# Early-fusion transformer block on one core: query and key products in two places a step, other PSUM banks for token values, contexts and projection

## The chip, the core and the metric

The kernel runs on one NeuronCore of a Trainium2 chip. TensorE (PE) multiplies matrices into PSUM, ScalarE (ACT) and VectorE (DVE) read PSUM and write SBUF, GpSimd (POOL) and SyncE (SP) mostly issue DMAs and do small work. Each engine runs its own instructions in order, and engines wait for one another through semaphores. The metric is the device time of one execution in microseconds; less is better.

## The reference

```python
h = tok(x)                       # 256x256 image, 3 channels: colour matrix, curve, mix, clip to 0..1
h = concat([h, txt], axis=1)     # 8 batches x 384 tokens x 256
h = h + attn(layernorm(h))       # 16 heads of 16, causal, latent keys and values
h = h + ffn(layernorm(h)) + bias # 8 experts, top 2, capacity 384 rows, gelu, 256 -> 1024 -> 256

def attn(x):
    c = x @ W_DKV                # latent, 64 wide
    k, v, q = c @ W_UK, c @ W_UV, x @ W_UQ
    s = q @ k.T * 0.25, masked causally
    return softmax(s) @ v @ W_O
```

## The kernel before

The program has two stages. The first (`front`) does tokens, attention and routing for 8 batches of 384 tokens; the second (`experts`) does the feed-forward part. The change is in `front` alone.

**Turns and steps.** A batch has 16 heads in two halves of 8. A turn `n` treats half `n % 2` of batch `n // 2`; it has four steps `p`, of two heads each. In a step PE computes, in this order: scores of the next turn for the row maxima, group 0 (L604, 8 matmuls with their masks), shifted scores of this turn unit 0 (L626), place A, shifted scores unit 1, scores group 1, the middle place, shifted scores unit 2, and the end place. ACT takes the exponential of each shifted unit (L917, L919), DVE reduces each group of scores to row maxima (L1111) and PE may not write a group again before DVE has read it. At places A, middle and end stands everything else, spread by hand over the steps: PE, ACT, DVE and SP each have a loop over `n` and `p` with the same ifs, and each engine's order is the order of the code. "Odd turn" and "even turn" below mean the parity of `n`.

**Queries and keys.** q and k are split in three bf16 parts each, so that their products can be taken exactly enough in bf16. `query_key(b, k, stage)` does it in three stages: stage 0 multiplies in fp32 (queries L720, `k` even; keys L722, `k` odd), ACT copies the result to `part` as bf16 (L978); stage 1 and 2 subtract the last part inside PSUM by a product with minus the identity (L725) and ACT copies again. So 12 products and 12 copies a batch make one chain, since from batch 2 on all use the same PSUM bank (`M[1]`, the third bank of `t_bank`): a product waits for the copy before it. In the code before, they stand in all three places of the steps: two of the chain in odd step 1, three each in odd steps 2 and 3 and in even step 0, the last in even step 1. SP sends each part on to the stacked tiles `qs` and `ks` (L392).

**The single banks.** `M[0]` (`bank0`) serves the transposes of the row maxima (`maxima`, L635), one half of the token values (L732, 2 tiles), contexts out of an odd turn (L681), the projection (`project`, L690) and the transposed rows for the router (`rows_back`, L740). `M[1]` serves tokens back (L698), latents (L705), the query and key chain, the other half of the token values (1 tile) and contexts out of an even turn. `take` makes PE wait until the last reader of a bank is done.

**Other work in the places.** ACT has colours (L953) in odd steps, relus (L962) in even steps 0 and 1; DVE has the rest of the colours, the token curve (L1162, L1166), norms, routing and residual additions (L1145).

Of the kernel before, what the change touches and what calls it, by code (L numbers as in the profile page):

```python
# [30 lines left out]
B = 8  # L31
# [110 lines left out]
def front(nc, common, lent, wr, w_in, routed, x, txt, params, mats, w1, w2, slot_rows, out):  # L142
# [8 lines left out]
    ident, banks, s_bank, t_bank, buf, sem = common  # L151
# [7 lines left out]
    def live(b):  # L159
        return 0 <= b < B  # L160
# [4 lines left out]
    def late(b):  # L165

        return 2 <= b < B
# [179 lines left out]
        return C[:, T:T + NT * KE] if b < B - 2 else s_bank[:, 1, 0:NT * KE]  # L347

    def project_bank(b, k):
        return s_bank[:, 2, :] if b == B - 1 and k else M[0]  # L350

    def rows_bank(b, c):
        return M[1] if b == B - 1 and c else M[0]
# [2 lines left out]
    EARLY_ORDER = (((0, 0), (1, 0), (2, 0), (0, 1), (1, 1), (3, 0), (0, 2), (1, 2), (2, 1), (3, 1), (2, 2), (3, 2)),  # L356
                   tuple((k, i) for half in ((0, 1), (2, 3)) for i in range(3) for k in half))
    EARLY_BANKS = (("s0", "s1", "s2", "t0"), (1, "C", 1, "C"))

    def bank_of(key):  # L360
        if key == "C":
# [32 lines left out]
    def sync(sp):  # L394
# [36 lines left out]
        for n in range(FIRST, LAST):  # L431
            b = n // 2
            if n % 2 == 0:
                if b + 1 == 1:
                    for i in range(3):
                        for k in (2, 3):
                            stack(sp, 1, k, i)
                elif live(b + 1):
                    for i in range(3):
                        stack(sp, b + 1, 3, i)  # L440
                if live(b + 2) and live(b + 4):
                    load_x(b + 4)
                if live(b - 2):
                    store(b - 2)
                if b + 2 == B:
                    sp.wait_ge(tok_done, B)
                    for i, w in enumerate(weight_layouts(w1, w2, 0)):
                        sp.dma_start(wr[i][:, :].rearrange("p (c f) -> p c f", f=w.shape[2]),
                                     w).then_inc(w_in[i], 16)
            else:  # L450
                if b + 2 == 1:
                    for i in range(3):
                        for k in (0, 1):
                            stack(sp, 1, k, i)
                    load_x(3)
                elif live(b + 2):
                    for k in range(3):
                        for i in range(3):
                            stack(sp, b + 2, k, i)
            if 0 <= n < PIECES:  # L460
                empty_rows(n)
# [121 lines left out]
    def tensor(pe):  # L583
        last = {}
# [58 lines left out]
        def take(bank, reader, count):  # L643

            release(bank)
            last[bank] = [(reader, count)]
# [36 lines left out]

        def project(b, k):
            pe.wait_ge(cn_sb, 2 * b + 2)
            take("last" if b == B - 1 and k else 0, hid_add, 2 * b + k + 1)
            dst = project_bank(b, k)
            for at, t in enumerate((0, 1) if k == 0 else (2,)):
                for c in range(KC):
                    mm = pe.matmul(dst[:, at * DIM:(at + 1) * DIM], cn[:, c, t * P:(t + 1) * P], wo[:, c, :],  # L690
                                   start=(c == 0), stop=(c == KC - 1))
            mm.then_inc(wo_ps, 1)
# [94 lines left out]
        for n in range(FIRST, LAST):  # L787
            b, odd = n // 2, n % 2
            nxt, cur, prev = turn_live(n + 1), turn_live(n), turn_live(n - 1)
            for p in range(4):  # L790
# [23 lines left out]
                        contexts_back(n, 0, False)  # L814
                if odd and p == 1 and late(b + 2):
                    latents(b + 2, 1)
                if odd and p >= 2 and late(b + 2):
                    query_key(b + 2, p - 2, 2)
                if not odd and p < 2 and late(b + 1):
                    query_key(b + 1, 2 + p, 2)  # L820

                if n == FIRST and p == 3:
                    for k in (0, 1):
# [10 lines left out]
                    for k in (2, 3):  # L834
                        query_key(1, k, 1)

                if odd and late(b + 2):
                    if p == 0:
                        tokens_back(b + 2, 0, 1)
                    else:  # L840
                        query_key(b + 2, p - 1, 0)
                if not odd and p == 0 and late(b + 1):
                    query_key(b + 1, 3, 0)
                if p == 0 and prev:
                    values(n - 1, 1)
                if p == 2 and cur:
# [1 line left out]
                if odd:  # L848
                    if p == 0 and live(b - 1) and n < OVER:
                        project(b - 1, 1)  # L850
                    if p == 3 and live(b - 1):
                        rows_back(b - 1, 0)
                else:
                    if p == 1 and live(b + 1):
                        token_values(b + 1, 0, 0)
                    if p == 3 and live(b - 1):
                        project(b - 1, 0)
                    if p == 3 and n == OVER:
                        ranks(b - 2)
                        project(b - 1, 1)  # L860
                        turning(50)
# [4 lines left out]
                if odd:  # L866
                    if p == 2 and prev:
                        contexts_out(n - 1, 0)
                    if late(b + 2):
                        if p == 0:  # L870
                            tokens_back(b + 2, 1, 1)
                        else:
                            query_key(b + 2, p - 1, 1)
                    if n == FIRST and p == 0:
                        for c in range(KC):
                            tokens_back(1, c, c)
# [5 lines left out]
                    if p == 3 and live(b - 1):  # L882
                        rows_back(b - 1, 1)
                else:
                    if p == 0 and late(b + 1):
                        query_key(b + 1, 3, 1)
                    if p == 1 and live(b + 1):
                        token_values(b + 1, 1, 1)
                    if p == 2 and prev:
                        contexts_out(n - 1, 1)  # L890
                        if n == OVER:
                            turning(20)
                    if n == OVER and p == 0:
# [6 lines left out]
    def scalar(act):  # L900
# [116 lines left out]
        for n in range(FIRST, LAST):  # L1017
            b, odd = n // 2, n % 2
            nxt, cur, prev = turn_live(n + 1), turn_live(n), turn_live(n - 1)
            for p in range(4):  # L1020
                if p == 3 and prev:
                    contexts_out(n - 1, 0 if odd else 1)
                if odd and p == 1 and late(b + 2):
                    tokens_back(b + 2, 1, 1)
                if odd and p >= 2 and late(b + 2):
                    query_key(b + 2, p - 2, 1)
                if not odd and p < 2 and late(b + 1):
                    query_key(b + 1, 2 + p, 1)
                if cur:
                    exps(n, p, 0)  # L1030

# [3 lines left out]
                    maxima(n + 1, 0)  # L1035
                if odd and p == 1 and late(b + 2):
                    latents(b + 2, 1)
                if odd and p >= 2 and late(b + 2):
                    query_key(b + 2, p - 2, 2)
                if not odd and p < 2 and late(b + 1):  # L1040
                    query_key(b + 1, 2 + p, 2)
                if n == FIRST and p == 3:
                    for k in (0, 1):
                        query_key(1, k, 1)
# [9 lines left out]
                if p == 2 and nxt:  # L1054
                    max_rows(n + 1, 0)

                if odd and late(b + 2):
                    if p == 0:
                        tokens_back(b + 2, 0, 1)
                    else:  # L1060
                        query_key(b + 2, p - 1, 0)
                if not odd and p == 0 and late(b + 1):
                    query_key(b + 1, 3, 0)
                if n == 0 and p == 0:
                    for k in (2, 3):
                        query_key(1, k, 1)
# [10 lines left out]
                    contexts(n - 1, 1)  # L1077
                if p == 2 and cur:
                    contexts(n, 0)
                if not odd and p == 0 and live(b + 2):  # L1080
                    relus(b + 2, 0)
                if not odd and p == 1 and live(b + 1):
                    token_values(b + 1, 0, 0)
                    token_values(b + 1, 1, 1)
                if n == FIRST and p == 0:
                    for c in range(KC):
                        tokens_back(1, c, c)
# [641 lines left out]
```

## Time and profile before

| what | value |
|---|---|
| time, median of 3 runs | 706.63 us (704.95 to 707.01) |
| profiled execution, its time | 704.81 us |
| profiled execution, its span | 703.1 us |
| PE busy | 639.8 us (91%) |
| DVE busy | 400.3 us (57%) |
| ACT busy | 377.8 us (54%) |
| POOL busy | 305.5 us (43%) |

The span is divided in two: attention up to some 380 us, experts from some 402 us on. The turns that hold a query and key chain of a late batch (2 to 7) lie between 60 and 320 us. In the rows of the timeline a row is one group of equal instructions; its second number is how long it was busy, and in brackets at its end stands how long the engine had been idle and what released it. The busy time of a matmul overlaps with the next one's.

### The profile page before, as it was taken

How to read it: one execution, taken by the hardware profiler on the slowest of the kernel's cores; microseconds unless marked ns; L12 is line 12 of the kernel's file. 1: busy time of each engine (PE TensorE's matmuls, PEld its weight loads, DVE VectorE, ACT ScalarE, POOL GpSimd, SP SyncE). 2: the span in 40 equal slices, each digit the busy share in tenths (PEclk: the TensorE clock that was granted, in tenths of full speed). 3: DMA queues.
4: the chain of work that ended last, by engine and by line, in shares of the span. 5: the costliest groups of instructions: out<-in, count | busy, mean ns of one | idle time of the engine just before them, and what ended most of it. 6: DMA issues, size and time to landing. Idle time of an engine off the chain costs nothing.

```text
span 703.1 us, 14382 instructions
## 1 busy us (share of the span) xinstructions
PE 639.8 (91%) x5488; PEld 533.9 (76%) x5488; DVE 400.3 (57%) x1005; ACT 377.8 (54%) x800; POOL 305.5 (43%) x415
## 2 busy tenths in 40 slices
PE   2799899998999999999988699999999999999991
PEld 2556565665666657567667699999999999999990
DVE  4887585687777877757766353444444444444310
ACT  4466766747667576565561265555555554555530
POOL 3300001004121141220426497888888888888222
PEclk9999999999999999999999889999999999999996
DMA  7448391714424043153103443444444444442222
GB/s 260 113 119 230 97 269 52 199 47 134 118 68 131 9 112 93 56 144 129 63 17 103 127 143 76 106 106 106 106 106 106 106 106 106 106 106 47 23 25 28
DMA packets 66477, 73.76 MB, mean 105 GB/s; under 512 B 6312, under 2 KB 61458, under 8 KB 66408
## 3 DMA queue, kind: packets, MB, share of 16 engines
q1 hardware_dynamic: 55584, 59.27, 27.8%
q0 software_dynamic: 9504, 13.00, 10.9%
q8 instruction: 44, 0.72, 0.5%
q10 hardware_dynamic: 1320, 0.57, 0.3%
q14 instruction: 25, 0.20, 0.1%
HBM read 31.62 MB, written 22.35 MB: 77 GB/s over the span
## 4 chain that ended last, share of the span: by engine, by line
PE 67%; DVE 12%; ACT 7%; issue 5%; DMA 3%; SPq 3%; POOL 1%; ACTq 0%; DVEq 0%; POOLq 0%
PE t_bank L1654 19%; PE bank L1669 12%; PE s_bank L1669 6%; PE bank L662 5%; DVE mx L1111 3%; PE t_bank L626 3%; PE t_bank L720 3%; SPq L392 3%; PE s_bank L604 3%; ACT part L978 2%; PE bank L690 2%; PE s_bank L1640 2%; DVE wr L1166 2%; PE t_bank L627 1%; PE s_bank L605 1%
## 5 line engine op out<-in xcount | busy, mean ns | idle before, releaser
L1613 DVE TENSOR_TENSOR hl<-h,hh 128x384 fp32r<-128x384 f32 x128 | 104.5, 818 | 155.7 <-ACT h L1571 155.7
L1111 DVE TENSOR_REDUCE mx<-s_bank 128x2 f32<-128x256 f32 (+2 forms) x192 | 122.6, 683 | 51.9 <-PE s_bank L605 51.3
L1568 ACT ACTIVATE hh<-t_bank 128x384 fp32r<-128x384 f32 x128 | 63.0, 492 | 133.9 <-PE t_bank L1654 131.7
L919 ACT ACTIVATE pt<-t_bank 128x512 f32<-128x512 f32 x128 | 76.8, 601 | 65.8 <-PE t_bank L627 64.8
L1538 POOL DMA_INDIRECT out<-yo,xr x48 | 75.0, 1564 | 72.6 <-ACT yo L1579 62.9
L1526 POOL TENSOR_TENSOR wl<-wr,wh 128x256 fp32r<-128x256 f32 x112 | 94.5, 878 | 1.2
L1654 PE MATMUL t_bank<-xh,wh 128*128 128x384 f32 x256 | 87.2, 341 | 0.0
L1654 PE MATMUL t_bank<-xl,wh 128*128 128x384 f32 x256 | 86.8, 339 | 0.0
L1654 PE MATMUL t_bank<-xh,wl 128*128 128x384 f32 x256 | 86.7, 338 | 0.0
L626 PE MATMUL t_bank<-qs,ks 98*128 98x384 bf16 (+2 forms) x384 | 85.2, 274 | 0.6 <-ACT pt L917 0.4
L604 PE MATMUL s_bank<-ks,qs 96*128 96x128 bf16 (+2 forms) x384 | 78.3, 273 | 5.4 <-DVE mx L1111 4.6
L520 POOL DMA_INDIRECT slot_rows<-row,slot_i x48 | 47.9, 997 | 73.9 <-ACT pt L919 47.7
L605 PE MATMUL s_bank<-mask_q,ident_b 128*128 128x128 bf16 x384 | 74.4, 219 | 0.0
L1669 PE MATMUL bank<-wh,hh 128*128 128x256 f32 x256 | 72.9, 285 | 0.0
L1669 PE MATMUL bank<-wh,hl 128*128 128x256 f32 x256 | 72.0, 281 | 0.0
L1669 PE MATMUL bank<-wl,hh 128*128 128x256 f32 x256 | 71.8, 280 | 0.0
L627 PE MATMUL t_bank<-mask_k,ident_b 128*128 128x128 bf16 x384 | 68.0, 219 | 0.0
L1571 ACT ACTIVATE h<-t_bank 128x384 f32<-128x384 f32 x128 | 62.3, 487 | 0.0
L626 PEld LDWEIGHTS t_bank<-qs,ks 98*128 98x128 bf16 x384 | 37.6, 98 | 24.0 <-issue 5.3
L502 POOL TENSOR_TENSOR ve<-mv,eps_t 128x3 f32<-128x3 f32 x8 | 1.5, 191 | 123.6 <-DVE mv L1201 123.6
L978 ACT ACTIVATE part<-t_bank 128x384 bf16<-128x384 f32 x78 | 38.1, 488 | 29.0 <-PE t_bank L720 16.9
L1654 PEld LDWEIGHTS t_bank<-xh,wh 128*128 128x128 f32 x256 | 49.4, 193 | 0.0
(191 smaller groups left out, 1433.6 us busy)
## 6 DMA issues: line engine op xcount, KB each, us to landing
wr<-in_w SPq DMA_DIRECT2D x16, 1024.0 KB, 5.7
qs<-part SPq DMA_DIRECT2D x96, 96.0 KB
ks<-part SPq DMA_DIRECT2D x90, 96.0 KB
slot_rows<-empty SPq DMA_DIRECT2D x4, 1560.0 KB, 9.3
xr<-slot_rows SPq DMA_DIRECT2D x16, 390.0 KB, 3.3
wr<-in_x SPq DMA_DIRECT2D x8, 768.0 KB, 5.4
out<-hid SPq DMA_DIRECT2D x8, 384.0 KB
qs<-mT ACTq DMA_DIRECT2D x64, 3.0 KB
```

Of the source, the lines that this page charges most:

```text
L604: pe.matmul(dst, q[0:MROW, h, j * P:(j + 1) * P], k[0:MROW, h, 0:w], start=True, stop=False)
L605: mm = pe.matmul(dst[:, j * P:(j + 1) * P], ident_b[:, :], mask_q[:, :], start=False, stop=True)
L626: pe.matmul(bank[:, col:col + w], k[:, h, j * P:(j + 1) * P], q[:, h, j * P:T], start=True, stop=False)
L627: mm = pe.matmul(bank[:, col:col + P], ident_b[:, :], mask_k[:, :], start=False, stop=True)
L919: ins = act.activation(pt[:, p, unit // 2, 0:AT[1]], bank, ACT.Exp)
L1111: ins = dve.tensor_reduce(mx[:, p // 2, j, 2 * (p % 2):2 * (p % 2) + 2], pair_region(s_bank, j), AX_X, ALU.max)
L1526: m = pool.tensor_tensor(wl[i][q][:, cols], wr[i][:, cols], wh[i][q][:, cols].bitcast(F32), ALU.subtract)
L1538: pool.indirect_dma_start(out=out, out_offset=bass.IndirectOffsetOnAxis(ap=xr[u % NX][:, t, DIM:DIM + 1].bitcast(I32), axis=0), in_=yo[u % ...
L1568: act.activation(hh[:, f, :], h_banks[f % NH], ACT.Gelu_apprx_tanh)
L1613: dve.tensor_tensor(hl[:, f, :], h[f % 2][:, :], hh[:, f, :].bitcast(F32), ALU.subtract).then_inc(hl_done, 1)
L1654: m = pe.matmul(h_banks[f % NH], w[:, c, cols], xx[:, c, :], start=(i == 0), stop=(i == len(parts) - 1))
L1669: m = pe.matmul(y_banks[t], hx[:, f, rows], w[:, f, :], start=(f == 0 and i == 0), stop=(f == FC - 1 and i == 2))
```

## The change

A function `ahead(n, p, place)` numbers the products of a chain over six steps: place 0 is place A, place 1 is the middle place. Odd step 1 has product 0 (middle), odd steps 2 and 3 and even steps 0, 1 and 2 have two each, even step 3 has the last (place A). The end place has none any more. ACT's copies follow: place 0 behind the exponential of unit 0, place 1 behind that of unit 1, none at the head of a step. Token values now both use `M[0]`: tile pair 0 at the end of even step 0, tile 2 in the middle of even step 1. Contexts out always use `M[0]`, the first half of each projection always `M[1]`. SP sends the parts of `k` 2 and 3 in the even turn, those of `k` 0 and 1 in the odd turn.

```diff
     def project_bank(b, k):
-        return s_bank[:, 2, :] if b == B - 1 and k else M[0]
+        if k == 0:
+            return M[1]
+        return s_bank[:, 2, :] if b == B - 1 else M[0]
...
+    def ahead(n, p, place):
+
+        b = n // 2 + (2 if n % 2 else 1)
+        i = 2 * p + place + (-3 if n % 2 else 5)
+        return (b, *divmod(i, 3)) if late(b) and 0 <= i < 12 else None
...
# sync
                 elif live(b + 1):
-                    for i in range(3):
-                        stack(sp, b + 1, 3, i)
+                    for k in (2, 3):
+                        for i in range(3):
+                            stack(sp, b + 1, k, i)
...
                 elif live(b + 2):
-                    for k in range(3):
+                    for k in (0, 1):
                         for i in range(3):
                             stack(sp, b + 2, k, i)
...
# tensor
-            take("last" if b == B - 1 and k else 0, hid_add, 2 * b + k + 1)
+            take(1 if k == 0 else "last" if b == B - 1 else 0, hid_add, 2 * b + k + 1)
...
-                if odd and p >= 2 and late(b + 2):
-                    query_key(b + 2, p - 2, 2)
-                if not odd and p < 2 and late(b + 1):
-                    query_key(b + 1, 2 + p, 2)
+                if ahead(n, p, 0):
+                    query_key(*ahead(n, p, 0))
...
-                if odd and late(b + 2):
-                    if p == 0:
-                        tokens_back(b + 2, 0, 1)
-                    else:
-                        query_key(b + 2, p - 1, 0)
-                if not odd and p == 0 and late(b + 1):
-                    query_key(b + 1, 3, 0)
+                if odd and p == 0 and late(b + 2):
+                    tokens_back(b + 2, 0, 1)
+                if ahead(n, p, 1):
+                    query_key(*ahead(n, p, 1))
...
-                        token_values(b + 1, 0, 0)
+                        token_values(b + 1, 1, 0)
...
-                    if late(b + 2):
-                        if p == 0:
-                            tokens_back(b + 2, 1, 1)
-                        else:
-                            query_key(b + 2, p - 1, 1)
+                    if p == 0 and late(b + 2):
+                        tokens_back(b + 2, 1, 1)
...
-                    if p == 0 and late(b + 1):
-                        query_key(b + 1, 3, 1)
-                    if p == 1 and live(b + 1):
-                        token_values(b + 1, 1, 1)
+                    if p == 0 and live(b + 1):
+                        token_values(b + 1, 0, 0)
                     if p == 2 and prev:
-                        contexts_out(n - 1, 1)
+                        contexts_out(n - 1, 0)
```

The same is done in ACT's loop (copies, token values, contexts out).

On ACT, this is what stands before in an odd turn from the first copy of the chain (step 1) to the contexts (step 2): `pt` is an exponential, `part01` the copy behind stage 1 of product group `k` = 0, `g` a colour, `mT` the row maxima, `cx` the contexts.

```order
L978 ACTIVATE part00<-t_bank 128x384
L919 ACTIVATE pt<-t_bank 128x512
L953 ACTIVATE g<-wr0,prm 128x512
L978 ACTIVATE part01<-t_bank 128x384
L919 ACTIVATE pt<-t_bank 128x512
L926 ACTIVATE mT<-bank0 8x384
L978 ACTIVATE part02<-t_bank 128x384
L917 ACTIVATE pt<-t_bank 128x2x256
L931 DMA qs00<-mT 1x4x384 x2
L978 ACTIVATE part10<-t_bank 128x384
L919 ACTIVATE pt<-t_bank 128x512
L939 ACTIVATE cx<-bank1 128x384
```

And this is what stands there now (the line numbers of ACT's code are one lower):

```order
L977 ACTIVATE part00<-t_bank 128x384
L918 ACTIVATE pt<-t_bank 128x512
L952 ACTIVATE g<-wr0,prm 128x512
L918 ACTIVATE pt<-t_bank 128x512
L925 ACTIVATE mT<-bank0 8x384
L977 ACTIVATE part01<-t_bank 128x384
L916 ACTIVATE pt<-t_bank 128x2x256
L930 DMA qs00<-mT 1x4x384 x2
L977 ACTIVATE part02<-t_bank 128x384
L918 ACTIVATE pt<-t_bank 128x512
L938 ACTIVATE cx<-bank1 128x384
```

The copy between the colour and the next step's first exponential is gone; the two others of the step are there still, and hold the members of the chain that stood one place earlier.

On PE, this is the order before from the middle place of even step 1 to the beginning of step 2: `L732` is a product of token values, `L626` and `L627` a shifted unit.

```order
L732 MATMUL bank0<-mat,ckvT 128x256 x2
L626 MATMUL t_bank<-qs10,ks10 128x384
L627 MATMUL t_bank<-mask_k,ident_b 128x128
L626 MATMUL t_bank<-qs10,ks10 128x128
L627 MATMUL t_bank<-mask_k,ident_b 128x128
L732 MATMUL t_bank<-mat,ckvT 128x256
L604 MATMUL s_bank<-ks11,qs11 128x128
```

And this is the order now (the line numbers of PE's code are nine higher):

```order
L734 MATMUL t_bank<-part21,minus_b 128x384
L741 MATMUL bank0<-mat,ckvT 128x256
L635 MATMUL t_bank<-qs10,ks10 128x384
L636 MATMUL t_bank<-mask_k,ident_b 128x128
L635 MATMUL t_bank<-qs10,ks10 128x128
L636 MATMUL t_bank<-mask_k,ident_b 128x128
L613 MATMUL s_bank<-ks11,qs11 128x128
```

The pair of token values has gone to the end of step 0, a subtraction of the chain stands in its place, and step 1 ends with the shifted unit.

## Rows read from the trace of the kernel before

**Rows 1.** The page: span, and TensorE's clock in 40 slices.
```profile
span 703.1 us, 14382 instructions
...
PEclk9999999999999999999999889999999999999996
```
**Rows 2.** Odd, even turn: length; busy PE, PEld, DVE, ACT, POOL; clock; DMA.
```profile
146.90:170.98 24.08, 21.65 (x197) 14.18 (x196) 17.27 (x60) 14.91 (x32) 6.26 (x8) 1.00 0.25 67
170.98:191.70 20.72, 19.75 (x198) 14.22 (x196) 16.55 (x47) 13.97 (x30) 4.06 (x5) 1.00 0.47 129
```
**Rows 3.** PE's waits from 60 to 400 us: total us, times, longest.
```profile
PE t_bank L725 <- ACT part L978: 5.5, 13, 0.7
PE t_bank L722 <- ACT part L978: 4.1, 12, 0.6
PE bank L635 <- DVE hid L1145: 3.6, 6, 0.7
PE s_bank L604 <- DVE mx L1111: 3.3, 5, 0.7
```
**Rows 4.** PE's waits from 30 to 60 us.
```profile
PE bank L635 <- ACT vb L987: 1.0, 1, 1.0
```
**Rows 5.** Timeline of PE and ACT, odd steps 1 and 2.
```profile
157.91 0.22 PE L627 MATMUL t_bank<-mask_k,ident_b 128*128 128x128 bf16 x1
158.22 0.59 ACT L919 ACTIVATE pt<-t_bank 128x512 f32<-128x512 f32 x1
158.38 0.34 PE L725 MATMUL t_bank<-part,minus_b 128*128 128x384 bf16 x1 [0.24 <-ACT part L978]
158.55 0.22 PE L604 MATMUL s_bank<-ks,qs 96*128 96x128 bf16 x1
158.69 0.81 ACT L953 ACTIVATE g<-wr,prm 128x512 f32<-128x512 f32 x1
159.40 0.49 ACT L978 ACTIVATE part<-t_bank 128x384 bf16<-128x384 f32 x1
...
160.12 0.60 ACT L919 ACTIVATE pt<-t_bank 128x512 f32<-128x512 f32 x1 [0.23 <-issue]
160.62 0.46 ACT L926 ACTIVATE mT<-bank 8x384 bf16<-8x384 bf16 x1
160.74 0.22 PE L605 MATMUL s_bank<-mask_q,ident_b 128*128 128x128 bf16 x1
160.99 0.46 ACT L978 ACTIVATE part<-t_bank 128x384 bf16<-128x384 f32 x1
161.59 0.88 PE L722 MATMUL t_bank<-ckvT,mat 128*128 128x384 f32 x2 [0.63 <-ACT part L978]
162.41 0.53 PE L662 MATMUL bank<-pt,vb 128*32 128x384 f32 x4
```
**Rows 6.** Timeline of DVE and PE at the beginning of an odd turn.
```profile
147.33 0.68 DVE L1145 TENSOR_TENSOR hid<-hid,bank 128x512 f32<-128x512 f32 x1
148.15 0.33 PE L635 MATMUL bank<-ident_b,ms 128*8 128x128 bf16 x3 [0.74 <-DVE hid L1145]
```
**Rows 7.** Timeline of PE and DVE in even steps 1 to 3.
```profile
180.05 1.08 PE L732 MATMUL bank<-mat,ckvT 128*128 128x256 f32 x4
180.97 0.33 PE L626 MATMUL t_bank<-qs,ks 98*128 98x384 bf16 x1
185.58 1.88 DVE L1111 TENSOR_REDUCE mx<-s_bank 128x2 f32<-128x256 f32 x3
186.93 0.23 PE L604 MATMUL s_bank<-ks,qs 96*128 96x128 bf16 x1 [0.69 <-DVE mx L1111]
```
**Rows 8.** Timeline of PE, the two transposes of rows, odd step 3.
```profile
169.26 0.49 PE L740 MATMUL bank<-ident,row 128*128 128x128 f32 x3
170.00 0.34 PE L725 MATMUL t_bank<-part,minus_b 128*128 128x384 bf16 x1
170.47 0.52 PE L740 MATMUL bank<-ident,row 128*128 128x128 f32 x3
```

More of the change, by code:

```diff
@@ L1021, in scalar @@
                 if p == 3 and prev:
-                    contexts_out(n - 1, 0 if odd else 1)
+                    contexts_out(n - 1, 0)
                 if odd and p == 1 and late(b + 2):
                     tokens_back(b + 2, 1, 1)
[L1025 to L1028, printed above, removed]
                 if cur:
@@ L1037, in scalar @@
                     latents(b + 2, 1)
[L1038 to L1041, printed above, removed]
+                if ahead(n, p, 0):
+                    query_key(*ahead(n, p, 0))
                 if n == FIRST and p == 3:
@@ L1055, in scalar @@
                     max_rows(n + 1, 0)
[L1057 to L1063, printed above, removed]
+                if odd and p == 0 and late(b + 2):
+                    tokens_back(b + 2, 0, 1)
+                if ahead(n, p, 1):
+                    query_key(*ahead(n, p, 1))
+                if not odd and p == 1 and live(b + 1):
+                    token_values(b + 1, 1, 0)
                 if n == 0 and p == 0:
@@ L1079, in scalar @@
                     contexts(n, 0)
+                if not odd and p == 0 and live(b + 1):
+                    token_values(b + 1, 0, 0)
                 if not odd and p == 0 and live(b + 2):
                     relus(b + 2, 0)
-                if not odd and p == 1 and live(b + 1):
-                    token_values(b + 1, 0, 0)
-                    token_values(b + 1, 1, 1)
                 if n == FIRST and p == 0:
```

## The prediction

> **What bounds the kernel now.** I read the page first: PE's clock stands at 9 tenths or more in every slice of attention [rows 1], so no pause there has cost clock. Then two stretches, one odd and one even turn of a late batch [rows 2]: PE is busy 21.65 of 24.08 us and 19.75 of 20.72, DVE 17.27 and 16.55, ACT 14.91 and 13.97. So PE sets the pace, DVE is the next, and what the change can give is at most the time in which PE waits. Then PE's waits between 60 and 400 us [rows 3]: 9.6 us in 25 waits for ACT's copies of the query and key chain (5.5 + 4.1), 3.6 us in 6 waits of the row maxima's transposes for DVE's residual addition, 3.3 us in 5 waits for DVE's maxima. One wait of 1.0 us for the token values of batch 1 stands before [rows 4].
>
> These sums are too small, since the modelled end of a matmul overlaps with the next start. The L627 at 157.91 is followed at a distance of 0.06 us when nothing holds PE, so L725 could have started at 157.97; it started at 158.38 [rows 5]. The wait is 0.41 us and the view says 0.24: add 0.17 to each wait. The Trainium skill, page "Perfetto Trace Analysis", section "Identifying the Most-Contended Engine", says in the same sense that matmul busy time misleads because instructions are pipelined; by busy time alone the 25 waits would be worth 9.6 us, by the distance of starts 13.9. By that rule the trace agrees (0.41 against 0.24).
>
> **The change, part by part.** Amount of work: every engine has the same products, copies and reductions as before, in other places; SP issues the same DMAs. The sum is therefore the waits that go less the waits that come.
>
> *Projection in the other bank.* In odd step 0 `maxima` needs `bank0`, in which the projection's first half lies until DVE has added it. The addition starts at 147.33, takes 0.68, and PE starts at 148.15 after 0.74 idle [rows 6]. Now that half is in `M[1]`. Six waits go: 3.6 + 6 x 0.17 = 4.6 us. `M[1]` is next wanted by tokens back in the middle place, behind a transpose and two more groups of products, when the addition is done. Late next is the projection itself: it needs the bank in which the last subtraction of the chain was made two groups of products earlier, and its copy. Subtraction to end of copy is about 0.9 us (L725 at 159.94 before its copy at 160.99 is held up by others, so I take 0.36 to start, 0.49 for the copy at 159.40 [rows 5], 0.07 to wake PE), the work between is 0.85: 0.07 each, 0.4 in all. Gain 4.2. Bounds: 0 (another wait takes its place) and 4.6.
>
> *The chain at odd step 2.* Work from the row of the last exponential of step 1, at 158.22, called X. Before, ACT has a colour at 158.69, a copy at 159.40, an exponential, `mT`, and the copy that PE needs at 160.99; PE goes on at 161.59. PE's last product ahead of it, L605 at 160.74, is followed at 0.06 us when free, so this wait is 0.79; and 0.41 was lost at 158.38 [rows 5]. Now ACT's line is exponential (0.47 to the colour), colour (0.71 to the next), exponential (0.50), `mT` (0.37), copy 0.46, and 0.11 until PE starts: X + 2.62. PE no longer subtracts at the end place; it needs 158.55 to 160.80 = 2.25 us for the same groups from 157.97 = X - 0.25, and is there at X + 2.00. It waits 0.62. Over six batches 3.7 us stay.
>
> *The chain at even step 0.* The same form (exponential, `mT`, copy). The mean wait of L722 is 4.1 / 12 + 0.17 = 0.51. ACT loses the copy at the step's head (about 0.40), PE the subtraction ahead of the step (L725 to L604, 158.38 to 158.55, 0.17 [rows 5]), so 0.51 - 0.40 + 0.17 = 0.28 stays: 1.7 us over six.
>
> *The rest of the chain.* From the middle place to place A of the next step lie a shifted unit, the next scores and another shifted unit, more than the 0.9 us that a copy takes; the waits at odd step 3 (the largest, 0.7 [rows 3]) go, because nothing is copied at the head of a step behind colour and contexts any more. From place A to the middle place lie a shifted unit and a group of scores: about 0.05 us each in 18 cases, 0.9 us. So the chain's waits go from 9.6 + 25 x 0.17 = 13.9 to 3.7 + 1.7 + 0.9 = 6.3: gain 7.6. Bounds: 3 (ACT is behind its line in every step, so that half of the pairs wait 0.5 us) and 13.9.
>
> *Even turns and DVE.* In even step 3 PE waits for maxima that DVE reads late (185.58), until 186.93, 0.69 + 0.17 = 0.86 us [rows 7]. DVE works on without a pause from the maxima of step 1 through routing and the token curve, so this time does not move with PE. PE arrives later by what has come between: less the pair of token values (180.05 to 180.97, 0.92 [rows 7]), plus two subtractions (0.17 each) and one key product (161.59 to 162.41, 0.82 [rows 5]), 0.24 us. Four of the five waits of [rows 3] lie in such turns: gain 1.0. Bounds: -1 (the curve comes later, since ACT's relus now stand behind one more copy; it has about 1.5 us to spare) and 3.4.
>
> *Rows back.* In odd step 3 the second transpose needs the copy of the first. They are 1.21 us apart (169.26, 170.47), and a subtraction at 170.00 fills 0.17 of it [rows 8]. That subtraction leaves, the distance stays: 5 x 0.17 = 0.9 us lost. Bounds 0 and -2.
>
> *Token values.* For batch 1 the wait of 1.0 + 0.17 [rows 4] goes, since tile 2's copy stands ahead of an exponential and not behind it; ACT is then later by 0.4: gain 0.7, bounds 0 and 1.2. For the others the bank is free a step ahead.
>
> *SP.* Parts of `k` = 2 are sent up to two steps later, the image load and the store wait behind them in the same queue. The stacked tile of `k` 2 and 3 is read a whole turn later (over 20 us [rows 2]), the image two turns later: 0. If one were late, some 2 us a batch.
>
> Sum: 4.2 + 7.6 + 1.0 - 0.9 + 0.7 = **12.6 us**. The profiled execution took 704.81 us (span 703.1 and 1.7 around it), so 692.2. The median of the runs is 706.63, 1.8 above it; I give the time from there: **694.0**.
>
> A place where the skill would say more: "TensorE: Matmul & The Clock Gate", section "A second HAM failure mode: psum-queue depth-cycling", tells of a kernel in which small pauses between groups in changing banks made the clock fall and rise, and by it fewer pauses would give back clock too. Here the clock is granted at 1.00 (2.4 GHz) in both stretches [rows 2] in spite of six or seven pauses in each pair, so the trace disagrees and nothing is added.
>
> **The rivals.**
> *ACT gives it back.* With two copies in a step beside three exponentials ACT may be behind at each place A. For it: ACT's line in rows 5 is full from 158.22 to 161.45. Against it: busy only 14.91 of 24.08. Then the chain keeps some 11 of its 13.9 us, and the gain is 4.2 + 3 - 1 = 6: 700.5.
> *All waits go.* PE's arrival in even step 3 is later than reckoned, and ACT is early: 4.6 + 11 + 3 = 18.5 less 1: 689 or a bit less. For it: each small wait ahead of step 3 hides in the one for DVE. Against it: ACT's line X + 2.62 is fixed by in-order work.
> *Slower: odd turns do not shrink.* The change moves two subtractions and a query product (0.17 + 0.17 + 1.37, the last estimated from twice the key product less the pause) from the odd into the even turn, 1.7 us. If the odd turn's length is set by DVE and ACT handing colours to each other and not by PE, it stays at 24.08 while the even turn, where DVE works without a pause, grows: 6 x 1.7 = 10.3, less the 1.5 that rows 6 and 7 leave: 715. It decides where DVE's 17.27 us meet the new length of the odd turn, 24.08 - 1.7 - 2.3 = 20.1; so 2.8 us of room speak against it.
> *No change.* The freed time is lost again before the experts' stage, which starts on routed rows that DVE, POOL and a DMA deliver in sequence: 706. Against it: this sequence starts from the last turn's products, and comes earlier with them.
>
> **How the numbers follow.** A measurement tells 0.3% (2.1 us) from no change. Forecast (690 to 698): 0.62; ACT gives it back (698 to 704): 0.15; all waits go (below 690): 0.09; no change: 0.06; slower: 0.08. Faster is 0.62 + 0.15 + 0.09 = 0.86, same 0.06, slower 0.08. The range 688 to 702 leaves out the slower case, no change and the edges of two others, some 0.2.
>
> **What would show it.** After the change: no wait of `maxima` for `hid`; a wait for ACT's copy at the middle place of odd step 2 of some 0.45 in the view, less than 0.2 elsewhere; a wait for DVE's maxima at even step 3 of some 0.45; a wait of 0.3 at the second rows back; odd turns near 20.2 us, even turns near 22.5, a pair near 42.7 (44.80 before). The prediction is wrong if odd turns stay above 22 us, if the waits for `part` sum to more than 8 us, or if ACT's exponentials hold PE at L626.

## The result, and the profile after

| | before | after |
|---|---|---|
| time, median | 705.79 us (703.58 to 707.01, 4 runs) | 694.45 us (692.97 to 694.65, 4 runs) |
| profiled execution, its time and span | 704.81, 703.1 us | 694.65, 692.9 us |
| ratio of the times | | 0.9845, 95% interval 0.9821 to 0.9869 |

The changed kernel is faster by 11.3 us in the medians and by 10.2 us from profile to profile. The page of its profiled execution, span and TensorE's clock, answers to [rows 1]:

```profile
span 692.9 us, 14382 instructions
...
PEclk9999999999999999999999899999999999999996
```

There are as many instructions as before and the clock stands as high: only waits can have gone. One odd and one even turn, with the columns of [rows 2]:

```profile
143.10:163.99 20.89, 20.09 (x198) 13.78 (x196) 17.55 (x57) 14.04 (x30) 6.45 (x8) 1.00 0.33 102
163.99:186.10 22.11, 21.32 (x200) 14.82 (x198) 17.63 (x52) 14.40 (x31) 4.06 (x5) 1.00 0.37 100
```

These stretches and those of [rows 2] are not cut at the same product: the odd stretch before starts behind the turn's first group of scores and the even one ends with the next turn's, while those above start and end at the first scores. From the first product of scores of one turn to that of the next (turns 5 and 6) it is 24.60 and 20.26 us before, 20.96 and 21.81 after. So the odd turn is shorter by 3.6 us, the even one longer by 1.55, the pair 42.77 for 44.86. DVE is now busy in 17.55 of 20.89 us of the odd turn, where it was in 17.27 of 24.08. PE's waits from 60 to 400 us, as in [rows 3] (total, times, longest):

```profile
PE s_bank L1631 <- DMA xr<-slot_rows: 6.1, 2, 3.6
PE bank L749 <- ACT rowT L990: 2.8, 7, 0.5
PE t_bank L734 <- ACT part L977: 2.3, 6, 0.4
PE t_bank L729 <- ACT part L977: 2.1, 6, 0.4
PE s_bank L613 <- DVE mx L1102: 1.6, 6, 0.5
```

The waits for ACT's copies of the chain (`part`) went from 9.6 us in 25 to 4.4 us in 12, the waits for `hid` are gone, those for the maxima `mx` fell from 3.3 to 1.6 us. (L1631 is the experts' first product, which waits for a DMA and now lies inside the window.) The waits of the transposed rows for their copy (`rowT`) grew; before, that row was

```profile
PE bank L740 <- ACT rowT L991: 0.8, 2, 0.5
```

What is left at odd step 2, against [rows 5]; columns are start, busy time, engine, line:

```profile
239.95 0.59 ACT L918 ACTIVATE pt<-t_bank 128x512 f32<-128x512 f32 x1
240.43 0.81 ACT L952 ACTIVATE g<-wr,prm 128x512 f32<-128x512 f32 x1
241.13 0.60 ACT L918 ACTIVATE pt<-t_bank 128x512 f32<-128x512 f32 x1
241.61 0.46 ACT L925 ACTIVATE mT<-bank 8x384 bf16<-8x384 bf16 x1
241.98 0.46 ACT L977 ACTIVATE part<-t_bank 128x384 bf16<-128x384 f32 x1
242.50 0.34 PE L734 MATMUL t_bank<-part,minus_b 128*128 128x384 bf16 x1 [0.40 <-ACT part L977]
```

From the exponential X = 239.95 ACT works without a gap, and PE goes on at X + 2.55 after 0.40 + 0.17 = 0.57 us. Even step 3, against [rows 7], and the two transposes of rows, against [rows 8]:

```profile
222.93 1.88 DVE L1102 TENSOR_REDUCE mx<-s_bank 128x2 f32<-128x256 f32 x3
224.27 0.23 PE L613 MATMUL s_bank<-ks,qs 96*128 96x128 bf16 x1 [0.23 <-DVE mx L1102]
...
247.90 0.49 PE L749 MATMUL bank<-ident,row 128*128 128x128 f32 x3
249.12 0.52 PE L749 MATMUL bank<-ident,row 128*128 128x128 f32 x3 [0.39 <-ACT rowT L990]
```

The wait for the maxima is 0.40 us where it was 0.86. The transposes are 1.22 us apart, as before (1.21), with no product of the chain between them.

**A mark in attention.** Two runs of one kernel differ by up to 3.5 us, most of it behind attention (last section). So I also compare each kernel by the start of the last transposes of row maxima (turn 15, step 0), a row that every kernel has. Before:

```profile
356.58 0.33 PE L635 MATMUL bank<-ident_b,ms 128*8 128x128 bf16 x3 [0.19 <-DVE hid L1145]
```

After:

```profile
346.28 0.33 PE L644 MATMUL bank<-ident_b,ms 128*8 128x128 bf16 x3
```

The gain at this mark is 10.3 us. The same transposes in each turn split it by pairs of turns (odd and following even): turns 1 and 2 gained 2.03, 3 and 4 2.03, 5 and 6 2.09, 7 and 8 1.84, 9 and 10 1.84, 11 and 12 0.50, turns 13 to 15 up to the mark 0.27. "Steady pair" means turns 9 and 10 below: 44.56 us before, 42.72 after.

The mark has a scatter of its own. Turn 1 starts 0.29 us later after the change than before, but so do the very first transposes of this kind (38.17 before, 38.47 after): it is not turn 0 that lost it. Ahead of them PE waits for a DMA, and that wait was 0.65 to 1.41 us long in the traces, also in kernels with the same code up to there. Before, and in `e_sp`:

```profile
32.54 0.22 PE L604 MATMUL s_bank<-ks,qs 96*128 96x128 bf16 x1 [0.83 <-DMA qs<-part]
33.27 0.22 PE L605 MATMUL s_bank<-ks,qs 96*128 96x128 bf16 x1 [1.41 <-DMA qs<-part]
```

From the first transposes to the mark the change gains 10.6 us. Counted so, the kernels of the next section gain over the one before: `e_bank` 4.3, `e_places` 8.95, `e_mt` 13.4, `e_sp` 0.1, `e_tv` 10.7, `e_curve` 12.3, `e_rows` 13.5, `e_all` 12.4, `e_best` 13.8, `e_dve` 16.8, `e_three` 7.9. Each is one trace.

### The profile page after: what moved, and what is told of

Its sections match the earlier page's. It is cut to its first block, busy times and chain, and to the rows that moved or that the text cites. A ratio compares the mean times of both kernels' runs of the same rounds, so it can differ in the third digit from the quotient of the medians.

```text
span 692.9 us, 14382 instructions
## 1 busy us (share of the span) xinstructions
PE 637.3 (92%) x5488; PEld 533.1 (77%) x5488; DVE 400.3 (58%) x1005; ACT 375.7 (54%) x800; POOL 306.7 (44%) x415
## 4 chain that ended last, share of the span: by engine, by line
PE 70%; DVE 8%; ACT 7%; issue 4%; DMA 4%; SPq 3%; POOL 2%; ACTq 1%; DVEq 0%; POOLq 0%
PE t_bank L1645 19%; PE bank L1660 12%; PE s_bank L1660 6%; PE bank L671 5%; PE t_bank L635 4%; PE s_bank L613 4%; PE t_bank L729 3%; SPq L400 3%; PE t_bank L699 2%; DMA qs<-part 2%; PE t_bank L636 2%; PE s_bank L614 2%; ACT part L977 2%; DVE mx L1102 2%; PE s_bank L1631 2%
## 5 line engine op out<-in xcount | busy, mean ns | idle before, releaser
L1604 DVE TENSOR_TENSOR hl<-h,hh 128x384 fp32r<-128x384 f32 x128 | 101.6, 794 | 158.1 <-ACT h L1562 158.1
```

The costliest lines, as they stand in the source:

```text
L1604: dve.tensor_tensor(hl[:, f, :], h[f % 2][:, :], hh[:, f, :].bitcast(F32), ALU.subtract).then_inc(hl_done, 1)
```

## The experiments

Each ratio is to the kernel before on the same chip (medians there 704.5 to 704.8 us), with its 95% interval. The mark is the row named above, 356.58 before and 346.28 after.

**The bank alone** (`e_bank`): the kernel before, with the projection's first half in `M[1]`.

```diff
     def project_bank(b, k):
-        return s_bank[:, 2, :] if b == B - 1 and k else M[0]
+        if k == 0:
+            return M[1]
+        return s_bank[:, 2, :] if b == B - 1 else M[0]
```

> The kernel before, with one part of the change: the first half of every projection in M[1], so that bank0 is free for the transposes of the row maxima at the head of an odd turn. Theory (six waits for DVE's residual addition go, each 0.60 us in the view and 0.17 more by the distance of starts): 4.6 us less than before, about 701.2 us against 705.8, ratio 0.9935, and no wait of L635 for hid. Rival (another wait takes its place in the same turn, since DVE is behind there without a pause): less than 1 us.

Measured: 701.13 us, ratio 0.995 (0.9931 to 0.9969), mark 352.33. It gains 4.25 at the mark, near the 4.6 expected, and the waits for `hid` are gone; the chain's stay (5.5 us in 13, 4.0 in 12), and so do those for the maxima (3.2 in 5). So it acts on that one wait.

**The places alone** (`e_places`): the changed kernel with the lines above undone.

> The changed kernel with that part undone: the chain in two places a step, token values and contexts as changed, but the projection's first half in bank0 again. Theory: the waits of the row maxima's transposes for hid come back, 0.6 to 0.8 us in each of six odd turns: 4 to 5 us more than the changed kernel, about 699 us, ratio to before 0.990. Rival (the two parts overlap: with the longer even turn DVE's addition is done in time, and the bank is worth little there): within 1 us of the changed kernel, 695.

Measured: 695.84 us, 0.9879 (0.9856 to 0.9902), mark 347.78. The places alone gain 8.8 us at the mark; the bank on top of them only 1.5. My expectation of 699 was wrong for that reason; the rival named beside it (695, the bank worth under 1 us) came nearer. Its waits:

```profile
PE bank L642 <- DVE hid L1134: 2.5, 5, 0.6
PE t_bank L732 <- ACT part L975: 2.3, 6, 0.4
PE t_bank L727 <- ACT part L975: 2.1, 6, 0.4
```

Five waits for `hid` are left, each shorter: in the steady pair 0.81 us before and 0.65 here, and at turn 3 0.54 before and 0.09 here (distances of starts). DVE's addition moves with the longer even turn, but PE comes later still: from the transposes at the start of the even turn to the addition it was 20.14 us before (281.31) and 21.46 here (273.21), and PE was free for its own next transposes 20.15 and 21.63 us behind the same point. At turn 3 these are 18.38 and 18.67 before, 19.23 and 19.95 here.

What the other banks of token values and contexts are worth inside the places was not run, except for batch 1 (`e_tv`).

**ACT's order** (`e_mt`): the changed kernel, with the copy that PE waits for ahead of the copy `mT` on ACT.

```diff
-                if p == 0 and cur:
-                    maxima(n, 1)
-                if p == 2 and nxt:
-                    maxima(n + 1, 0)
...
                     query_key(*ahead(n, p, 0))
+                if p == 0 and cur:
+                    maxima(n, 1)
+                if p == 2 and nxt:
+                    maxima(n + 1, 0)
```

> The changed kernel with one order on ACT turned: the copy of the chain's product of place A stands ahead of the copy of the row maxima (mT) and not behind it, in odd step 2 and even steps 0 and 2. Theory (what is left of the chain's waits is ACT's line exponential, mT, copy): the copy is 0.37 us earlier in each of 12 places where PE waits 0.57 and 0.52 us now, so 4.4 us less than the changed kernel, about 690 us, and the waits for part fall to 0.2 us or out of the view. Rival (DVE sets the turn now): PE only waits later for DVE's maxima, less than 1 us gained. Second rival: the row maxima's DMAs come 0.5 us later and hold the shifted scores: slower.

Measured: 691.16 us, 0.9799 (0.978 to 0.9819), mark 343.50. No other kernel of the study that computes everything was faster by the median (`e_rows` is level with it). It gains 2.8 us at the mark and 3.3 by the median over the change, where 4.4 were expected. All 12 waits for `part` left the list of 60 to 400 us, and others came:

```profile
PE s_bank L613 <- DVE mx L1102: 2.9, 8, 0.5
PE bank L749 <- ACT rowT L990: 2.8, 7, 0.5
...
PE bank L683 <- ACT cx L938: 1.3, 3, 0.5
```

The maxima hold PE for 1.6 us more (1.3 in the view and two waits more at 0.17), the contexts for 1.1 more. The list hides that the chain's pauses are shorter and not gone. By the distance of starts, those of more than 0.12 us ahead of the chain's products fell from 9.5 us in 29 to 4.0 in 23; in the steady pair the two large ones went from 0.57 and 0.52 to 0.23 and 0.17, that in even step 2 (0.28) fell below 0.12, and the pair shrank by 0.37. 5.5 - 1.6 - 1.1 = 2.8, the gain at the mark. So the copies behind `mT` were on the path, and the waits for DVE's maxima and for ACT's copies of contexts take back a half.

**SP's order alone** (`e_sp`): the kernel before, with the parts of `k` 2 sent in the even turn.

```diff
-                    for i in range(3):
-                        stack(sp, b + 1, 3, i)
+                    for k in (2, 3):
+                        for i in range(3):
+                            stack(sp, b + 1, k, i)
```

> The kernel before with SP's part of the change alone: it sends the parts of k = 2 in the even turn, ahead of those of k = 3, and the image load and store behind them. Theory: nothing reads the stacked tile or the image for a turn, so no change, ratio 1.000 within 0.002. Rival (a DMA lands late): about 1 us or more slower.

Measured: 704.45 us, 0.9991 (0.998 to 1.0002), mark 356.99: no change. The 0.4 us at the mark comes from the longer wait ahead of turn 0 shown above; from the first transposes on it is 318.27 us for 318.41.

**Token values of batch 1** (`e_tv`): the changed kernel, with these products and copies in turn 0 where and in the banks that they had before.

```diff
                     if p == 1 and live(b + 1):
-                        token_values(b + 1, 1, 0)
+                        if n == 0:
+                            token_values(b + 1, 0, 0)
+                        else:
+                            token_values(b + 1, 1, 0)
...
```

> The changed kernel with the token values of batch 1 alone where they were (turn 0, step 1, two banks). Theory from the traces: in turn 0 ACT works without a pause from 50 to 57 us, so its work sets the time there and the order of its copies is worth nothing: 0.0, within 0.3 us of the changed kernel (694.5), with the wait of 1.0 us for vb back and the waits for exponentials (0.76 and 0.52) gone. The prediction's term would make it 0.7 us slower.

Measured: 694.68 us, 0.9859 (0.9843 to 0.9875), mark 345.98: the same as the change. From the first transposes to those of turn 1 it is 24.21 us before and here, 24.20 with the change. From 30 to 60 us it has the old wait again, `vb` for 1.0 us:

```profile
PE bank L644 <- ACT vb L991: 1.0, 1, 1.0
...
PE t_bank L635 <- ACT pt L923: 0.2, 1, 0.2
```

The changed kernel has in the same stretch:

```profile
PE t_bank L635 <- ACT pt L916: 0.8, 1, 0.8
...
PE t_bank L635 <- ACT pt L918: 0.5, 1, 0.5
```

The wait changed its name. ACT works there without a gap, so PE is paced by it in either order (rows of the changed kernel):

```profile
54.02 0.64 ACT L916 ACTIVATE pt<-t_bank 128x512 f32<-128x512 f32 x1
54.50 0.44 ACT L986 ACTIVATE vb<-bank 128x256 f32<-128x256 f32 x1
54.76 0.79 ACT L961 ACTIVATE r<-g,minus_s 128x512 f32<-128x512 f32 x1
55.38 1.15 ACT L918 ACTIVATE pt<-t_bank 128x512 f32<-128x512 f32 x2
```

**DVE's curve later** (`e_curve`): `e_mt`, with the token curve behind the maxima of even step 2.

```diff
-                    if p == 1 and live(b + 2):
+                    if p == 2 and live(b + 2):
                         curve(b + 2)
                         curve_rest(b + 2)
...
```

> The changed kernel with mT behind the chain's copy (as in e_mt, 691.2 us), and on DVE the token curve one step later: behind the maxima of even step 2 and not ahead of them. Theory (DVE's curve of about 2.9 us is what makes PE wait at even step 3, 0.61 us by the distance of starts in e_mt, six times): 2 to 3 us less than e_mt, about 688.5 us. Rival (DVE's total work since even step 1 sets the time, so the wait only moves to odd step 0): as e_mt. What would make it slower: the curve ends later, and with it xn and the tokens back.

Measured: 693.65 us, 0.9852 (0.9838 to 0.9866), mark 344.43: slower than `e_mt` by 0.9 at the mark, where a gain was expected. The steady pair went from 42.36 to 42.13 us; but turn 0 grew from 16.96 to 18.66 us, since the longest wait for the maxima there became 1.7 us. And a new wait took most of the gain of the steady pairs:

```profile
PE s_bank L613 <- DVE mx L1102: 2.9, 5, 1.7
...
PE t_bank L707 <- DVE hid L1136: 1.0, 5, 0.2
```

**Rows back earlier** (`e_rows`): `e_mt`, with the first transposes of rows ahead of the chain's product at the middle place.

```diff
+                if odd and p == 3 and live(b - 1):
+                    rows_back(b - 1, 0)
                 if ahead(n, p, 1):
                     query_key(*ahead(n, p, 1))
...
```

> e_mt with the first transpose of rows for the router ahead of the chain's product in the middle place of odd step 3, and its copy likewise. PE waits 0.55 us at the second transpose there in e_mt, and 0.41 us for DVE's maxima right behind it (even step 0). Theory (DVE's maxima of odd step 3, behind the colours, hold the next turn): the first wait goes and the second grows by as much, so less than 0.7 us gained, 690.7. Rival (PE's wait is worth its length): 5 x 0.55 = 2.7 us gained, 688.5.

Measured: 691.19 us, 0.9816 (0.9799 to 0.9834), mark 343.26 (343.50 in `e_mt`): 0.2 us, and less than 0.1 from the first transposes on, as the theory had it. The wait left ACT's copy and went to DVE:

```profile
PE s_bank L613 <- DVE mx L1102: 4.4, 9, 0.7
...
PE bank L749 <- ACT rowT L990: 1.7, 7, 0.5
```

**All three** (`e_all`): `e_mt` with the last two edits together.

> e_mt, e_curve and e_rows together. Theory: the sum of e_curve and e_rows, 2 to 3.5 us less than e_mt, about 688 us, and PE's waits for DVE's maxima at even step 0 are what is left. Rival (with both, DVE is nowhere caught up, and the waits for maxima come back in every turn): no better than e_curve.

Measured: 695.07 us, 0.9866 (0.9847 to 0.9884), mark 344.35: no better than `e_curve` (344.43), where 688 us was expected and the rival named this. The median is also 1.4 us above `e_curve`'s; in the profiled runs the difference lies behind the mark (last section).

**The curve later, except in turn 0** (`e_best`).

```diff
-                    if p == 2 and live(b + 2):
+                    if p == (2 if n else 1) and live(b + 2):
                         curve(b + 2)
                         curve_rest(b + 2)
```

> e_curve with the curve of batch 2 (turn 0) left in step 1, where it was. The trace of e_curve shows 1.7 us lost in turn 0 and 0.2 us won in each pair of turns, so the attention part should end 0.8 us earlier than in e_mt: 690.4 us, a difference about as large as what can be measured.

Measured: 692.07 us, 0.9811 (0.9797 to 0.9825), mark 343.23. Turn 0's loss is gone, but against `e_mt` (343.50) the gain is 0.3 at the mark, 0.4 from the first transposes on, and none in the median.

**Less work for DVE** (`e_dve`): `e_mt`, with DVE's colours and curve on 8 of 256 columns from batch 3 on; it leaves most of these values out.

```diff
+            w = 8 if b >= 3 else W
-            dve.scalar_tensor_tensor(out=g[:, d, :, :], in0=xin[b % 2][:, c, :, :],
+            dve.scalar_tensor_tensor(out=g[:, d, :, 0:w], in0=xin[b % 2][:, c, :, 0:w],
...
```

> e_mt with VectorE's colours and curve on 8 columns of 256 for batches 3 to 7, so most of their values are left out. Theory (after the change DVE is what PE waits for: 0.61 us at even step 3 and 0.41 at even step 0 by the distance of starts): these waits go in four or five pairs of turns, 4 to 5 us less than e_mt, about 686.5 us, and no wait for mx from 100 us on. Rival (PE's own work sets the turns, the waits are only passed on to ACT's copies): within 1 us of e_mt.

Measured: 688.24 us, 0.9765 (0.9752 to 0.9778), mark 339.88, 3.6 us ahead of `e_mt` (3.4 from the first transposes on, 2.9 by the median; 4 to 5 were expected). The waits for the maxima are what went, from 2.9 + 8 x 0.17 = 4.3 us to 0.7:

```profile
PE s_bank L613 <- DVE mx L1102: 0.5, 1, 0.5
```

So DVE's work is what takes back part of each gain once the chain's waits are short; here that is worth 3.4 to 3.6 us.

**Three places, ACT's order** (`e_three`): the kernel before, with the bank and ACT's order of `e_mt`. Is it the number of places that matters, or only where the copy stands on ACT?

> The kernel before with three places a step kept, the projection in the other bank (e_bank, 701.1 us) and on ACT the chain's copy ahead of mT. If the number of places did not matter and only ACT's line, this would reach the changed kernel, 694.5. Theory: the copy is 0.37 us earlier in 12 places, 4.4 us at most, and the waits at the end place (0.41 us) and at odd step 3 (0.85 us) stay: 697 us, 2.5 us above the changed kernel.

Measured: 696.99 us, 0.9889 (0.9871 to 0.9907), mark 348.83:

```profile
PE t_bank L727 <- ACT part L980: 5.5, 13, 0.7
...
PE t_bank L724 <- ACT part L980: 0.3, 1, 0.3
```

ACT's order takes the waits for the copy of place A's product out of the list but for one (L724, in the middle place, 4.0 us in `e_bank`), while the 13 waits at the end place and at the place A behind it stay at 5.5 us. The time is what was expected. With the same bank for the projection and the same order on ACT, two places (`e_mt`) are 5.3 us ahead of three at the mark; they also have the token values and contexts in their new banks. Both the places and the order count.

## Why the prediction was right, and where its size was off

**Time and direction.** 694.0 was forecast and 694.45 measured. The closeness flatters the sum: from profile to profile I reckoned 12.6 us and 10.2 came (10.3 at the mark, 10.6 from the first transposes on); 1.8 us had been added for the median of the kernel before, which later runs put at 704.5 to 704.8. That the two cancel is luck.

**What was off** is the sum: it took the bank's 4.2 us in full beside the places' 8.4 (7.6 + 1.0 - 0.9 + 0.7). Taken alone, each part comes out near its size, 4.25 and 8.8 us measured. But the bank is worth 1.5 and not 4.2 on top of the places: 12.6 - 2.7 + 0.4 = 10.3. The traces show where it goes. These are PE's pauses from the transposes of turn 1 to the mark, in us, each as its distance of starts less the distance that such a pair has when nothing holds PE (0.06 us behind a mask, 0.15 from there to a transpose of maxima); those over 0.03 us are summed:

| pauses ahead of | before | `e_bank` | `e_places` | after |
|---|---|---|---|---|
| the chain's products | 16.1 | 16.0 | 10.0 | 10.0 |
| the maxima's transposes (most of it for `hid`) | 4.4 | 0.4 | 3.0 | 0.1 |
| scores (the maxima) | 4.1 | 4.1 | 3.2 | 3.3 |
| the transposed rows (`rowT`) | 2.0 | 2.0 | 3.2 | 3.2 |
| the router's product | 1.0 | 1.0 | 0.3 | 0.3 |
| the projection | 0 | 0 | 0 | 0.9 |
| the whole stretch | 294.2 | 290.0 | 285.3 | 283.6 |

So the places alone take 1.4 us of the pauses ahead of the maxima's transposes (1.1 of it waits for `hid`), which the sum had given to the bank in full. And the projection's wait for `M[1]`, behind the chain's copy, exists only where both edits meet: 0.15 us in each of six turns, 0.9 and not 0.4. In a steady pair the pauses of `e_places` and of the changed kernel are the same but for these two: 0.65 us for `hid` goes and 0.15 us comes; net 0.50, and the pair shrank by 0.46. In turns 1 and 2 only 0.09 us for `hid` was left to win, and the projection (0.15) and tokens back, which use `M[1]` too (0.30 for 0.11), cost more: 0.26 us lost. I had given 0.07 to the projection and nothing to tokens back.

The places' total came out near its size by luck. The chain gave 6.1 us and not 7.6, the maxima 0.8 for 1.0, rows back took 1.2 for 0.9, token values gave nothing for 0.7. The pauses ahead of the maxima's transposes (1.4) and of the router's product (0.7), which the sum of the places did not have, made up for it. The rows of the table account for 9.8 of the 10.6 us; the rest is not located.

**The pairs of turns are not alike.** My 11.9 us without batch 1 are 2.0 for each of six pairs. Five gave 1.84 to 2.09, the sixth (turns 11 and 12) 0.50. The trace of the kernel before shows why, and I could have read it there. PE's waits in the steady pair:

```profile
PE t_bank L725 <- ACT part L978: 0.9, 2, 0.7
PE bank L635 <- DVE hid L1145: 0.7, 1, 0.7
PE s_bank L604 <- DVE mx L1111: 0.7, 1, 0.7
PE t_bank L722 <- ACT part L978: 0.6, 2, 0.3
```

and in turns 11 and 12 (the wait for `hid` stands at the very start of each stretch):

```profile
PE bank L635 <- DVE hid L1145: 0.7, 1, 0.7
PE t_bank L722 <- ACT part L978: 0.7, 2, 0.4
PE t_bank L725 <- ACT part L978: 0.2, 1, 0.2
```

There is no later batch whose tokens ACT and DVE must work on, so the large wait at odd step 3 (0.85 us in the steady pair) is 0.15 and the one for the maxima does not exist. There was little to win.

**The other steps.**
- Waits for `hid`: gone, as forecast; 4.2 reckoned, 4.25 alone.
- Odd step 2: 0.62 us forecast, 0.57 measured, PE on at X + 2.55 for X + 2.62. Right.
- Even step 0: 0.28 forecast, 0.52 measured (0.36 in the view). Wrong by 0.24, and in the wrong direction: it was 0.41 there before. The 0.51 that I started from was the mean of all twelve waits of L722, and those at odd step 2 are the longer ones (0.50 against 0.41 in the steady pair).
- The twelve large waits of the chain together: 3.7 + 1.7 = 5.4 us forecast, 4.4 + 12 x 0.17 = 6.4 measured.
- Small pauses between place A and the middle place in the three other steps: 0.05 each forecast; in the steady pair 0.17 (odd step 3), under 0.1 (even step 1) and 0.28 (even step 2). They lie below what the list shows. The 13.9 us before had left such small ones out (0.15 twice in each pair), so before and after were not counted alike.
- Maxima at even step 3: 0.6 forecast, 0.40 measured, from 0.86. Twice the gain reckoned for a turn. A new pause of 0.21 us for them stands at even step 0.
- Rows back: the distance stayed (1.22 for 1.21), as forecast; 0.9 us lost was forecast, 1.2 measured.
- Token values of batch 1: 0.7 forecast, 0 measured (`e_tv`), since ACT is full there. That "ACT is then later by 0.4" stood in the working; it had to be asked who waits for ACT.
- SP: 0 forecast, 0 measured (`e_sp`).
- Turns: 20.2 and 22.5 us forecast, from the stretches of [rows 2], which are not whole turns. From first scores to first scores it is 20.96 and 21.81. The forecast changes were -3.9 and +1.8, the measured ones -3.6 and +1.55. The pair was forecast near 42.7 and is 42.77.

All pauses of 0.09 us or more in the steady pair, by the distance of starts, sum to 4.6 us before and 3.2 after. That is 1.4 of the 1.84 us gained; 0.4 is not located.

**The rivals.** "ACT gives it back" (700.5): the waits for `part` fell below 8 us, so no. "All waits go" (689): no; even in `e_mt`, where the chain's waits leave the list, those for DVE's maxima grow from 1.6 to 2.9 us. "Slower": the odd turn shrank by 3.6 us; DVE's 17.55 us still had room. "No change": the experts' first products start 9.3 us earlier (400.34 before, 391.01 after). The clock was granted at 1.00 in both stretches before and after, with pauses of up to 0.9 us before and 0.6 after, so fewer pauses gave nothing back by the clock.

## What to carry to other kernels

Two waits on the same engine, removed by two edits, need not be worth their sum. One edit can shorten the other's wait by bringing the engine later to it (1.4 us of 4.4 here), and a bank that was free before can be taken in the new order (0.9 us). Reckon the second edit in the order that the first one leaves. Before multiplying one turn's gain by the number of turns, list the waits of the first and the last of them apart. Where the engine that is waited for is never idle, another order of its work moves the wait to another of its copies and gains nothing (`e_tv`). A view of waits with a lower bound hides pauses that add up: compare distances of starts, before and after alike.

## What the runs showed of the hardware that I had not expected

At the passage from attention to the experts TensorE is granted half its clock (0.5, so 1.2 GHz) for stretches whose sum differs between runs. The columns are those of [rows 2]. Before, one stretch of 10.2 us fills this window; PE had waited 3.10 us for a DMA up to 400.34:

```profile
400.00:410.00 10.00, 7.68 (x28) 7.31 (x29) 3.22 (x3) 6.42 (x9) 4.84 (x2) 0.51 0.68 226
```

After, there were two shorter ones, each inside one of these windows: 3.4 us behind PE's waits for the router's rows (1.51 and 0.63 us), and 6.8 us behind and about its waits for the experts' rows (3.61 and 2.53 us). Between them the clock was 1.00:

```profile
374.00:379.00 5.00, 4.91 (x55) 4.65 (x55) 3.15 (x27) 2.12 (x3) 3.78 (x5) 0.66 0.54 180
392.00:399.00 7.00, 4.58 (x17) 4.58 (x18) 1.91 (x2) 5.59 (x7) 4.22 (x1) 0.52 0.92 313
```

Over the thirteen traces the sum of these stretches goes with the time from the mark to the end. At 10.2 us (seven traces, the two above among them) it is 346.2 to 346.6 us; at 13.7 (`e_bank`, `e_tv`, `e_best`) 347.1 to 347.7; at 17.1 (`e_sp`, `e_all`) 348.2 and 348.4; at 6.8 (`e_dve`, whose values differ) 344.9. The runs of one kernel differ in the same way: of 17 runs of the kernel before on one chip, three with a mean granted clock of 0.987 took 703.4 to 703.9 us and four with 0.981 took 706.1 to 706.9. So most of the difference between runs goes with the granted clock, and from trace to trace with this passage. That is why the mark is the better measure, once the wait ahead of turn 0 is taken off: the kernel before and `e_sp` then differ by 0.14 us, the changed kernel and `e_tv` by 0.13.

A second thing: the pause that the view of waits gives for a product is shorter than the distance of starts says by 0.17 us behind a product of 128 columns (0.24 against 0.41 at 158.38 [rows 5]), and its list leaves out those that it takes for less than some 0.2 us. In the steady pair after the change these sum to 1.2 us by the distance of starts (0.10, 0.15, 0.17, 0.21, 0.10, 0.28 and 0.15), beside 1.5 us in the three waits for ACT and DVE that are listed for the chain and the maxima. The prediction says that the Trainium skill, page "Perfetto Trace Analysis", section "Identifying the Most-Contended Engine", speaks in the same sense. That section is about nearness to the peak and says that pipelined instructions look smaller in a trace; in these rows they look longer than the distance of their starts (0.22 us against 0.06 for L627 at 157.91 [rows 5]), so here the trace does not bear it out.
